# Second adapter's output product: from 256-column products with the two parts side by side to 128-column products that add them in the bank

## The reference

```python
x = x + (x @ W.T + 2.0 * sum_e gate_e * ((x @ A0_e.T) @ B0_e.T))
B_req, A_req = B1[adapter_ids], A1[adapter_ids]     # ids are per batch of 32 tokens
Bx  = einsum('bni,bri->bnr', x, B_req)              # "down": 512 -> 16
out = einsum('bnr,bor->bno', Bx, A_req)             # "up": 16 -> 512
x = x + out
```

## Time and profile before

| | |
|---|---|
| median of 3 runs | 107.45 us (106.88, 107.45, 107.86) |
| span of the profiled execution | 104.8 us |
| median less that span | 2.65 us |
| PE busy | 93.5 us, 733 products |
| PEld (weight loads) busy | 78.2 us, 733 loads |
| DVE busy | 68.0 us |
| ACT, POOL busy | 43.7 us, 39.0 us |

### The profile page before, as it was taken

How to read it: one execution, slowest core, us unless ns; L and a number is a source line. 1 busy time by engine, 2 the same in 40 slices (tenths; PEclk the granted TensorE clock), 3 DMA queues, 4 the chain that set the end, 5 groups by cost and what they waited for, 6 DMA issues and landing times.

```text
span 104.8 us, 2166 instructions
## 1 busy us (share of the span) xinstructions
PE 93.5 (89%) x733; PEld 78.2 (75%) x733; DVE 68.0 (65%) x220; ACT 43.7 (42%) x88; POOL 39.0 (37%) x42
## 2 busy tenths in 40 slices
PE   5999995009999999999999999999999999999970
PEld 2597882008799788988898888888988888898860
DVE  1269989994421997498604983988029839891890
ACT  3472604405693069802970489009803840000300
POOL 4002986996920000699900004998000072000000
PEclk9999999965599999999999999999999999999997
DMA  2999807426993693222569200222600002314046
GB/s 36 356 348 291 362 19 181 131 62 113 422 276 95 126 356 72 59 55 58 145 154 324 104 0 0 100 100 47 260 0 0 3 0 69 137 52 149 6 168 232
DMA packets 14989, 14.33 MB, mean 137 GB/s; under 512 B 10114, under 2 KB 11394, under 8 KB 14594
## 3 DMA queue, kind: packets, MB, share of 16 engines
q1 hardware_dynamic: 14050, 11.82, 35.1%
q0 software_dynamic: 640, 2.10, 7.2%
q10 hardware_dynamic: 288, 0.28, 1.1%
HBM read 9.99 MB, written 4.19 MB: 135 GB/s over the span
## 4 chain that ended last, share of the span: by engine, by line
PE 87%; issue 7%; DVE 3%; DVEq 0%
PE main L631 15%; PE main L637 14%; PE main L643 14%; PE aw_ps L673 12%; PE side L725 5%; PE main L658 3%; PE main L657 3%; PE main L659 3%; PE aw_ps L749 3%; PE main L772 3%; PE side L673 2%; DVE xs L520 2%; PE side L705 2%; PE main L749 1%; PE side L749 1%
## 5 line engine op out<-in xcount | busy, mean ns | idle before, releaser
L309 POOL TENSOR_TENSOR x_lo<-xs,x_hi 128x512 fp32r<-128x512 f32 x12 | 15.0, 1284 | 25.7 <-ACT x_hi L329 25.7
L631 PE MATMUL main<-x_hi,w_hi 128*128 128x512 f32 (+1 forms) x64 | 18.6, 414 | 0.0
L637 PE MATMUL main<-x_hi,w_lo 128*128 128x512 f32 (+1 forms) x64 | 17.7, 400 | 0.0
L643 PE MATMUL main<-x_lo,w_hi 128*128 128x512 f32 (+1 forms) x64 | 17.0, 387 | 0.0
L637 PEld LDWEIGHTS main<-x_hi,w_lo 128*128 128x128 f32 x64 | 12.4, 197 | 2.8
L673 PE MATMUL aw_ps<-aws,xs 128*128 128x136 f32 x112 | 14.1, 279 | 0.0
L643 PEld LDWEIGHTS main<-x_lo,w_hi 128*128 128x128 f32 x64 | 12.1, 192 | 2.6
L673 PEld LDWEIGHTS aw_ps<-aws,xs 128*128 128x128 f32 x112 | 13.7, 190 | 0.2
L631 PEld LDWEIGHTS main<-x_hi,w_hi 128*128 128x128 f32 x64 | 11.8, 197 | 2.5 <-DVE w_hi L543 0.2
L361 ACT ACTIVATE a_ops<-a_hi 64x512 fp32r<-64x512 f32 x12 | 7.6, 630 | 10.7 <-POOL a_rest L293 10.6
L479 DVE TENSOR_TENSOR xs<-main,xs 128x512 f32<-128x512 f32 x15 | 9.9, 683 | 2.8 <-PE main L659 2.8
(11 more groups left out here) (111 smaller groups left out, 145.8 us busy)
## 6 DMA issues: line engine op xcount, KB each, us to landing
out_t<-xs SPq DMA_DIRECT2D x16, 256.0 KB, 2.3
xs<-x_t SPq DMA_DIRECT2D x3, 1024.0 KB, 6.4
b1s<-b_t SPq DMA_DIRECT2D x64, 32.0 KB, 2.0
xs<-x_t SPq DMA_DIRECT2D x4, 256.0 KB, 4.2
ws<-w_t SPq DMA_DIRECT2D x4, 256.0 KB, 5.6
b0s<-b_t SPq DMA_DIRECT2D x1, 256.0 KB, 5.6
aws<-aw_t ACTq DMA_DIRECT2D x1, 204.0 KB, 4.0
rows<-a_t,row_at POOLq DMA_INDIRECT x8, 4.0
```

Of the source, the lines that this page charges most:

```text
L309: nc.gpsimd.tensor_tensor(x_lo[:, t % 2, c], xs[:, t, c], x_hi[:, t % 2, c].bitcast(F32), ALU.subtract).then_inc(x_lo_ready, 1)
L631: nc.tensor.matmul(out_ap, w_hi[:, c, k], x_hi[:, s, k, n], start=(k == 0), stop=False)
L637: nc.tensor.matmul(out_ap, w_lo[:, c, k], x_hi[:, s, k, n], start=False, stop=False)
L643: last = nc.tensor.matmul(out_ap, w_hi[:, c, k], x_lo[:, s, k, n], start=False, stop=False)
```

## The change

A part is now a whole chunk c of both groups: 512 tokens, one bank. For each group s and each half h, two products of 128 columns are issued with the same weights `a1_ops[:, a, h, m]`. The first has the rounded columns (0 to 127) of `down_ops` as its moving operand and starts the accumulation. The second has the columns of the rest (128 to 255) and adds to the same 128 columns of the bank. So the bank holds the finished sum for 512 tokens. One addition of 128 x 512 puts it into `xs`.

There are four parts in a block in place of eight, in the banks main 3, side 0, aw_ps 0 and aw_ps 1. All four stand where the first five stood, and the three late parts are gone. `x2_ready` and `up_done` count four steps a block.

```diff
-        PARTS = K * GPB
-        up_banks = main[2:] + side[:1] + aw_ps + side[:1] + aw_ps
-        EARLY = 5
+        UP = GT // 2
+        up_banks = [main[K - 1], side[0], aw_ps[0], aw_ps[1]]
...
-            def add_x2(t, parts):
-
-                def one(i, part):
-                    c, s = divmod(i, GPB)
-                    to = xs[:, t, c, s * GT:(s + 1) * GT].rearrange("p (h n) -> p h n", h=2)
-                    return nc.vector.tensor_tensor(
-                        to, up_banks[i][:].rearrange("p (h q n) -> p h q n", h=2, q=2)[:, :, part], to, ALU.add)
-                for i in parts:
-                    dve.wait_ge(up_done, t * PARTS + i + 1)
-                    last = one(i, 0)
-                then_wait(last)
-                for i in parts:
-                    one(i, 1).then_inc(x2_ready, 1)
+            def add_x2(t, c):
+                dve.wait_ge(up_done, t * K + c + 1)
+                nc.vector.tensor_tensor(xs[:, t, c], up_banks[c][:], xs[:, t, c], ALU.add).then_inc(x2_ready, 1)
...
-                    if c == 2 and t >= 1:
-
-                        add_x2(t - 1, range(EARLY, PARTS))
-
...
-                    for i in range(0, EARLY, 2):
-                        add_x2(t, range(i, min(i + 2, EARLY)))
+                    for c in range(K):
+                        add_x2(t, c)
...
                 if t >= 1:
-                    if c < 2:
+                    if main[c] in up_banks:
+                        pe.wait_ge(x2_ready, (t - 1) * K + up_banks.index(main[c]) + 1)
+                    else:
                         pe.wait_ge(x1_ready, (t - 1) * K + c + 1)
-                    else:
-                        pe.wait_ge(x2_ready, (t - 1) * PARTS + c - 1)
...
-                for h in range(2):
-                    last = nc.tensor.matmul(bank[:, h * GT:(h + 1) * GT], a1_ops[:, a, h, c * P:(c + 1) * P],
-                                            down_ops[:, a, h], start=True, stop=True)
+                for s in range(GPB):
+                    g, a = t * GPB + s, (t * GPB + s) % SLOTS
+                    if c == 0:
+                        pe.wait_ge(a1_packed, g + 1)
+                        pe.wait_ge(down_hi_ready, 2 * g + 2)
+                        pe.wait_ge(down_lo_ready, g + 1)
+                        pe.wait_ge(pads_ready, 2)
+                    for h in range(2):
+                        to = bank[:, s * GT + h * UP:s * GT + (h + 1) * UP]
+                        nc.tensor.matmul(to, a1_ops[:, a, h, m], down_ops[:, a, h, 0:UP], start=True, stop=False)
+                        last = nc.tensor.matmul(to, a1_ops[:, a, h, m], down_ops[:, a, h, UP:GT], start=False,
+                                                stop=True)
...
                 base(t + 1, 1)
-                for i in range(EARLY):
-                    up(t, i)
+                for c in range(K):
+                    up(t, c)
                 lora(t + 1, 0)
                 lora(t + 1, 1)
                 base(t + 1, 2)
-                for i in range(EARLY, PARTS):
-                    up(t, i)
                 lora(t + 1, 2)
```

More of the change, by code:

```diff
@@ L240, in _ @@
                 for c in range(K):
-                    sp.wait_ge(x2_ready, t * PARTS + (c + 1) * GPB)
+                    sp.wait_ge(x2_ready, t * K + c + 1)
                     sp.dma_start(out[:, t, c, :], xs[:, t, c, :]).then_inc(stored, 16)
@@ L246, in _ @@
                 for c in range(2, K + 1, 2):
-                    sp.wait_ge(x2_ready, (NB - 1) * PARTS + s * K + c)
+                    sp.wait_ge(x2_ready, (NB - 1) * K + s * K + c)
                     sp.dma_start(out[:, NB - 1, c - 2:c, n], xs[:, NB - 1, c - 2:c, n]).then_inc(stored, 16)
@@ L284, in split_a1 @@
                 if g >= SLOTS:
-                    pool.wait_ge(up_done, PARTS * (g // GPB - 1))
+                    pool.wait_ge(up_done, K * (g // GPB - 1))
                 s = g % SLOTS
@@ L346, in a1_half @@
                 if g >= SLOTS:
-                    act.wait_ge(up_done, PARTS * (g // GPB - 1))
+                    act.wait_ge(up_done, K * (g // GPB - 1))
                 s = g % SLOTS
@@ L518, in add_x2_last @@
                 n = slice(s * GT, (s + 1) * GT)
-                dve.wait_ge(up_done, (NB - 1) * PARTS + s * K + c + 1)
+                dve.wait_ge(up_done, (NB - 1) * K + s * K + c + 1)
                 nc.vector.tensor_tensor(xs[:, NB - 1, c, n], last_banks[s * K + c][:, 0:GT], xs[:, NB - 1, c, n],
                                         ALU.add).then_inc(x2_ready, 1)
-            def add_x2(t, parts):
-                def one(i, part):
-                    c, s = divmod(i, GPB)
-                    to = xs[:, t, c, s * GT:(s + 1) * GT].rearrange("p (h n) -> p h n", h=2)
-                    return nc.vector.tensor_tensor(
-                        to, up_banks[i][:].rearrange("p (h q n) -> p h q n", h=2, q=2)[:, :, part], to, ALU.add)
-                for i in parts:
-                    dve.wait_ge(up_done, t * PARTS + i + 1)
-                    last = one(i, 0)
-                then_wait(last)
-                for i in parts:
-                    one(i, 1).then_inc(x2_ready, 1)
+            def add_x2(t, c):
+                dve.wait_ge(up_done, t * K + c + 1)
+                nc.vector.tensor_tensor(xs[:, t, c], up_banks[c][:], xs[:, t, c], ALU.add).then_inc(x2_ready, 1)
             nc.vector.memset(zeros[:], 0.0).then_inc(zeros_ready, 1)
@@ L661, in base_last @@
             def base_last(s):
-                pe.wait_ge(x2_ready, (NB - 2) * PARTS + (K - 2 if s == 0 else PARTS - 1))
+                pe.wait_ge(x2_ready, (NB - 2) * K + up_banks.index(last_x1_banks[s]) + 1)
                 base_products(NB - 1, K - 1, last_x1_banks[s][:, 0:GT], slice(s * GT, (s + 1) * GT))
@@ L689, in aw_tiles @@
                 if u >= 2:
-                    pe.wait_ge(x2_ready, (u - 1) * PARTS)
+                    pe.wait_ge(x2_ready, (u - 1) * K)
                 for j in range(TILES):
@@ L721, in down_part @@
                     elif t >= 1:
-                        pe.wait_ge(x2_ready, t * PARTS)
+                        pe.wait_ge(x2_ready, t * K)
                 for j in range(CT):
@@ L729, in down_part, with up @@
                     last.then_inc(down_done, 1)
[L731 to L741, removed]
+            def up(t, c):
+                bank, m = up_banks[c], slice(c * P, (c + 1) * P)
                 if bank in main:
                     pe.wait_ge(x1_ready, t * K + main.index(bank) + 1)
-                if i >= EARLY:
-                    pe.wait_ge(x2_ready, t * PARTS + up_banks.index(bank) + 1)
-                for h in range(2):
-                    last = nc.tensor.matmul(bank[:, h * GT:(h + 1) * GT], a1_ops[:, a, h, c * P:(c + 1) * P],
-                                            down_ops[:, a, h], start=True, stop=True)
+                for s in range(GPB):
[10 more added lines that the diff above has]
+                                                stop=True)
                 last.then_inc(up_done, 1)
```

## The result

| | before | changed |
|---|---|---|
| median, us | 107.45 | 111.73 |
| lowest to highest | 106.21 to 107.86 | 111.12 to 113.08 |
| ratio, 95% interval | | 1.044 (1.037 to 1.051) |

A second comparison on one chip, 6 runs against 17 of before, gave 111.70 against 106.56 us, ratio 1.045 (1.041 to 1.049), or +4.8 us by the ratio. Some executions of either kernel fall into a slower state, and the ratios here leave them out, so they can differ a little from the quotient of the medians. The prediction said 113.1 us, in a range from 109.3 to 118.8.

The account below looks back on a forecast made before the run. TensorE's ordered work was taken to bound the kernel. Three blocks' short products add 5.66 us, all else 0: span 104.8 + 5.7 = 110.5 us, plus 2.65 between span and median gives 113.1 us, range 109.3 to 118.8.

Parts of the forecast that it names:

- What bounds the kernel: From about 30 to 92 us TensorE's ordered work sets the time; what is added to that stream adds to it.
- The prediction's own test of the mechanism: At "up": a 3.8 us stretch with a block period growing by less than 1.9 would mean an unseen wait was lifted.
- The price of a short product: In "up", each 128-column product costs 0.118 us: 3.78 us a block, +1.89 us; three blocks, +5.66 us.
- Two passes for an fp32r load: In "up", a weight load occupies the load path for two passes, 107 ns of its 188.
- D: In "up", short fp32r products run at the float32 rate: 0.226 us each, +16.0 us, 123.5 us; chance 9%.
- Same weights twice: In each "up" pair, the second product with the same weights still needs its own load; every load is counted.
- VectorE: Additions of "up" fall from 6.7 to 2.7 us a block, 11.8 us in all, costed at nothing.
- The order: All 32 "up" products at the early place bring no new wait: cost 0, and 0 gained.
- A: In "up", only columns count or the second load is free: time stays 107.45 us; 8% no difference, 3% faster.
- B: In "up", the load binds only in part: 0.088 us a product, +2.8 us, 110.3 us; chance 4%.
- C: In "up", load and product run in sequence: 0.177 us a product, +11.3 us, 118.8 us; chance 5%.

Follow-up runs that it names:

- the wide-product kernel: Changed kernel with one 256-column product in place of each pair of 128-column ones; 106.33 against 106.56 us for the kernel before, ratio 0.998 in twelve runs.

## Why the prediction was right

**What bounds the kernel.** Right. PE has no gap in any stretch with "up", before or after, and the times follow from the stretches: 3 x (3.53 - 1.89) = 4.9 us for the changed one (+4.8 measured) and 3.1 for the one with mixed types (+3.1). For the two with short loads the stretches give +0.1 and -0.4 us, and +0.4 (-0.1 to +0.9) was measured for each. The prediction's own test of the mechanism is met as well: the period of a block grows by 1.66 us, as much as its stretch.

**The price of a short product.** The mechanism was right, the size 6 to 7% too high. I took 0.118 us, the distance of the pair as it stood, and measured is 0.111 (0.110 with the first one). In the kernel before, load and stream were both 107 ns, and the row could not show that the 11 ns on top belong to the stream of 256 columns; a distance set by the load alone has only 4 ns on top. That is 0.25 us a block and 0.74 us of the 1.4 us by which 113.1 was too high. The rest is no term of the sum: three blocks of +1.64 make 4.9, and the two comparisons give +4.3 and +5.1 by their medians, +4.7 and +4.8 by their ratios; the prediction's base, 107.45 us, was above what the kernel before took in the later comparisons (106.2 to 106.6). The prediction also says that a load of 107 ns would add "+5 us or more"; it is 3 x (32 x 0.107 - 1.89) = +4.6, nearer to the measured growth than the +5.66 of the sum.

**Where the inference came from.** Two passes for an fp32r load were inferred from durations (188 against 140 ns, 330 against 188 at the two clocks). The load of half the columns, 136 ns, and the distances of 0.111 us at the full clock and 0.21 at the low one bear them out. The trace of before had another row for it: the router's float32 instructions, 136 columns (57 ns at 2.4 GHz) with a load each, follow at 0.113 us, much as the short products do here. The prediction used that row only for rival *D*. It fits a load as the bound; no run changed that product, so this is not shown.

**Same weights twice.** Right: 781 loads for 781 products, and no difference between pairs with the same and with different weights.

**VectorE.** Its relief was rightly costed at nothing; the wide-product kernel shows it (0.998). Its size was overstated: busy time fell by 8.6 us to 59.4, not by 11.8. Additions in a row overlap, four of them in 1.55 us, so the sum of their durations counts time twice: the 48 additions of before keep VectorE busy for 17.6 us and not for 20, and the twelve that replace them for 8.3. The last addition ends 0.89 us after "up" (47.63 and 46.74), as worked out.

**The order.** No new wait appeared: from 30 to 96 us PE is busy for 66.00 of 66.00.

**The rivals.** *A*, columns alone, is excluded by 64 and 192 columns at one distance, and a free second load by the counts. *B*, a load that binds in part, would have shown 0.088; it binds in full. The Trainium skill ("TensorE: Matmul & The Clock Gate", Back-to-back issue gap) has 81 ns for such a stream at 128 columns; measured are 111 ns in fp32r and 55 in bf16, so neither type agrees with it. *C*, in sequence, would have shown 0.177. *D* would have shown 0.226, and a rate by column would have grown from 64 to 192. In the stretches with "up" the clock stayed at 1.00 with 128 columns; that it can fall there was seen only with 64.

A version faster than both kernels did not come out of this. A wide product costs 0.118 us with one load; two short ones cost 0.222 with two. The form that would keep the single addition and the single load, one 256-column product whose halves add to the same 128 columns of the bank, was not tried. By the wide-product run it would only have brought the time of before.

## What to carry to other kernels

In a stream of products of one type, a product costs here the longer of its own columns and the weight load of the product behind it: 0.111 us at 64, 128 and 192 columns, 0.118 at 256. For 4-byte fp32r weights of 128 columns that load is 107 ns at the full clock, as long as 256 columns; splitting a product below that width buys loads and nothing else, even if the number of columns stays the same. Before work is moved from VectorE to TensorE, look at who waits for whom: here VectorE was idle behind TensorE before and after, so its saved microseconds had no buyer.

## What the runs showed of the hardware that was not expected

- A product's record can start before its weights are loaded. Its duration is then longer (0.27 to 0.28 us in place of 0.23 for 128 columns, 0.45 in place of 0.39 for 512), and distances between single starts mislead where neighbours differ; the distance over a whole pair or stretch does not.
- The granted clock fell to 0.50 in a stretch without idle time, near the end of 32 products of 64 columns with a full load each. That was in one profiled run, at the second of three such stretches (and behind the third); two of five runs had so low a mean clock. With 128 columns and the same loads it stayed at 1.00.
- At the low clock the distance of these products was 0.21 us in place of 0.11: the load of fp32r weights takes the same cycles at both.
- Alternating fp32r and bf16 products took 0.187 us a pair where the loads account for 0.167.
